# Moving one chunk of a key and value projection ahead of the output projection, and its k sums ahead of a residual and a norm

## The reference

```
x = x + xattn(ctx, layernorm(x), mask)
x = x + ffn(layernorm(x))

# xattn: latents l = layernorm(layernorm(x)), c = layernorm(ctx)
q    = l @ W_q
k, v = concat([c @ W_kv, l @ W_kv])        # 77 + 256 = 333 keys
qn, kn = rmsnorm(q) * scale, rmsnorm(k)    # per head of 64, 4 heads
attn = softmax(mask(qn @ kn.T)) @ v
out  = attn @ W_out + b_out

# ffn: shared part of 512 hidden units and 8 experts of 128, of which the router takes 2
out  = relu(x @ shared_up.T)**2 @ shared_down.T + sum_e w_e * relu(x @ up_e.T)**2 @ down_e.T
```

## Time and profile before

| | |
|---|---|
| median of 3 runs | 1163.17 us (1162.99 to 1163.61) |
| profiled execution, its own time | 1166.36 us |
| profiled execution, span of its instructions | 1164.6 us |
| PE busy | 1149.4 us (99% of the span) |
| DVE busy | 1005.6 us (86%) |
| ACT busy | 800.1 us (69%) |
| POOL busy | 542.9 us (47%) |
| mean granted TensorE clock | 0.994 |

### The profile page before, as it was taken

One profiled execution on the slowest core, in us unless ns is written; L12 is line 12 of the kernel. 1 busy time (PEld: TensorE's weight loads), 2 busy tenths in 40 slices (PEclk: granted clock), 3 DMA queues, 4 the chain that ended last, 5 costly groups with the idle time before them and its releaser, 6 DMA issues. The chain is left out here.

```text
span 1164.6 us, 32989 instructions
## 1 busy us (share of the span) xinstructions
PE 1149.4 (99%) x11772; PEld 1074.1 (92%) x11772; DVE 1005.6 (86%) x3511; ACT 800.1 (69%) x1896; POOL 542.9 (47%) x466
## 2 busy tenths in 40 slices
PE   7999999999999999999999999999999999999997
PEld 7799999999999999999999999999999999999997
DVE  6788888889988889988888988889888899888887
ACT  6567776676866667766677766678766678666673
POOL 3344545444545444445445444445454445454432
PEclk9899999999999999999999999999999999999999
DMA  5000000000000000000000000000000000000000
GB/s 186 2 14 23 23 23 11 23 14 24 22 23 10 23 14 22 24 22 11 14 23 23 23 19 16 13 22 23 22 12 22 14 23 22 23 10 24 2 10 19
DMA packets 28145, 26.06 MB, mean 22 GB/s; under 512 B 6544, under 2 KB 27440, under 8 KB 27984
## 3 DMA queue, kind: packets, MB, share of 16 engines
q1 hardware_dynamic: 27904, 23.83, 6.6%
q0 software_dynamic: 80, 0.14, 0.0%
HBM read 15.57 MB, written 8.39 MB: 21 GB/s over the span
## 5 line engine op out<-in xcount | busy, mean ns | idle before, releaser
L1311 POOL TENSOR_TENSOR hid_lo<-relu,hid_hi 128x512 fp32r<-128x512 f32 x191 | 246.7, 1292 | 251.8 <-DVE hid_hi L1069 167.2
L295 PE MATMUL down_ps<-down_hi,hid_hi 128*128 128x256 f32 x768 | 234.2, 305 | 2.8 <-DVE acc L1091 2.6
L1091 DVE SCALAR_TENSOR_TENSOR acc<-down_ps,route_w,acc 128x256 f32<-128x256 f32 x512 | 221.8, 475 | 6.9 <-PE down_ps L297 6.2
L295 PE MATMUL up_ps<-x_hi,up_hi 128*128 128x256 f32 x768 | 227.5, 296 | 0.0
L297 PE MATMUL down_ps<-down_hi,hid_lo 128*128 128x256 f32 x768 | 216.6, 282 | 0.0
L296 PE MATMUL down_ps<-down_lo,hid_hi 128*128 128x256 f32 x768 | 216.1, 281 | 0.0
L296 PE MATMUL up_ps<-x_lo,up_hi 128*128 128x256 f32 x768 | 214.9, 280 | 0.0
L297 PE MATMUL up_ps<-x_hi,up_lo 128*128 128x256 f32 x768 | 214.7, 280 | 0.0
L676 ACT ACTIVATE probs<-masked,neg_max,q_scale 128x333 f32<-128x333 f32 x256 | 168.1, 658 | 1.1 <-DVE neg_max L930 1.1
L723 ACT ACTIVATE relu_sb<-up_ps 128x512 f32<-128x512 f32 x192 | 113.6, 592 | 72.8 <-PE up_ps L297 69.5
L295 PEld LDWEIGHTS down_ps<-down_hi,hid_hi 128*128 128x128 f32 x768 | 144.9, 189 | 15.6 <-issue 15.1
(11 more groups left out here) (148 smaller groups left out, 2838.7 us busy)
## 6 DMA issues: line engine op xcount, KB each, us to landing
out<-acc SPq DMA_DIRECT2D x31, 256.0 KB, 2.2
x_first<-in_x SPq DMA_DIRECT2D x16, 256.0 KB, 2.8
w_stage<-in_x SPq DMA_DIRECT2D x16, 256.0 KB, 2.8
up_stage<-in_up_t SPq DMA_DIRECT2D x1, 1536.0 KB, 6.4
down_stage<-in_down_t SPq DMA_DIRECT2D x1, 1536.0 KB, 7.9
c_first<-in_ctx SPq DMA_DIRECT2D x16, 77.0 KB
w_stage<-in_ctx SPq DMA_DIRECT2D x16, 77.0 KB
w_stage<-in_w_kv SPq DMA_DIRECT2D x1, 512.0 KB, 5.0
```

Source lines behind the costliest of these rows:

```text
L295: nc.tensor.matmul(out_ap, s_hi, m_hi, start=first, stop=False)
L1091: nc.vector.scalar_tensor_tensor(acc[:, t, :], down_ps[:, (e + 1) % 2, t * D:(t + 1) * D], route_w[:, t, e:e + 1], acc[:, t, :], ALU.mult, ...
L1311: nc.gpsimd.tensor_tensor(hid_lo[:, p % HID_RING, :], relu2[:, p % 2, :], hid_hi[:, p % HID_RING, :], ALU.subtract).then_inc(hid_lo_done, 1)
```

## The change

On TensorE chunk 2 of the keys and values of the next element is projected directly behind chunk 1, ahead of both halves of the output projection. On DVE `k_norms` part 0 moves ahead of the two residual halves and the second norm's statistics. On POOL `k_scales` part 0 moves ahead of `rstd_second`. No instruction is added or removed, no DMA is moved, and ACT's order stays as it is.

```diff
@@ TensorE, step
                 ffn("down", 5)
                 project_kv(b + 1, 1)
+                project_kv(b + 1, 2)
                 project_out(b, 0, following)
                 project_out(b, 1, following)
-                project_kv(b + 1, 2)
                 project_kv(b + 1, 0)
                 project_q(b + 1)
                 ffn("down", 6)
@@ DVE, step
                 add(5)
                 if first:
                     down_parts(2)
+                k_norms(b + 1, 0, False)
                 residual_half(b, 0)
                 residual_half(b, 1)
                 layer_norm2(b, first)
-                k_norms(b + 1, 0, False)
                 normalize2(b, first)
                 k_norms(b + 1, 1, False)
@@ POOL, step
                     ln_low(b + 1)
                 low(5)
+                if following:
+                    k_scales(b + 1, 0, False)
                 rstd_second(b, first)
                 if following:
-                    k_scales(b + 1, 0, False)
                     k_scales(b + 1, 1, False)
```

## The result

The changed kernel takes 1199.41 us (1198.73 to 1199.88, 4 runs) against 1163.33 us for the kernel before (4 runs): a ratio of 1.0303, 95% interval 1.0290 to 1.0315. It is 36 us slower; 1195.0 was predicted, with a range of 1180 to 1206. On another chip, with more runs of the kernel before beside it, the same two stood at 1198.61 and 1164.57, ratio 1.0296 (1.0281 to 1.0311), 34 us.

A forecast was written before the change was run, and what follows sets the result against it. TensorE's in-order stream was taken to bound the kernel, the change acting only through late operands: 1.03 us in each of 31 steps, 32 us in all, gave 1195 us, range 1180 to 1206.

The forecast's parts named there:

- TensorE's order costs nothing by itself: On TensorE, out starts 1.38 us later and kv 2 1.55 earlier; the sum of its own work is unchanged, price nothing.
- The chain: K sums, residual, `var`, `rstd`, `x_hat`, part 1's k sums, `k_scale`, `k_rms` across DVE and POOL: TensorE 1.03 us late per step.
- The handover times: Signal delays between engines, 0.04 to 0.13 us for each of five handovers, uncertain by 0.25 us per step.
- The first wait: TensorE at `transpose_x2` waits for `x_hat`, starting 0.58 us late in each step.
- the second: TensorE at `transpose_k`'s fifth transpose waits for `k_rms` part 1: 1.03 us late, the wait at `transpose_x2` included.
- The first step: The step of `b` = 0, with its own 1.24 us wait for `k_rms`, charged the same 1.03 us as the others.
- the clock as a rival for each step: New TensorE waits halve the granted clock each step, 1.7 us per stretch, 51 us on top, 1246 us; 5%.
- The sum: Over the whole span, 31 steps at 1.03 us make 32 us, taken from the profiled execution to the median: 1195.2 us.
- only the first wait is paid: `k_rms` comes before TensorE needs it, so only `transpose_x2`'s 0.58 us per step is paid: 1181 us; 7%.
- POOL's results come before its records end: On POOL, 1.03 us of `rstd` and part 1's `k_scale` is only record, so time stays at 1163 us; 6%.
- The Trainium skill's rule on DVE's handovers: DVE's next instruction starts only once the pipeline ahead is empty: 0.17 us later per step, 5 us more, 1200 us.

The follow-up runs named there:

- POOL's order of before: Changed kernel with `rstd` put back ahead of both `k_scale` on POOL: 1205.19 us, ratio 1.0352 to the kernel before.
- both with the k sums between the halves: Changed kernel with part 0's k sums between the two residual halves: 1212.76 us; the same with `rstd` back ahead of `k_scale` on POOL: 1210.07 us.
- DVE's and POOL's parts alone: Kernel before with only the DVE and POOL moves of the change, TensorE's order kept: 1241.35 us, ratio 1.0654.
- POOL's alone: Kernel before with only `k_scale` part 0 moved ahead of `rstd` on POOL: 1226.26 us, ratio 1.0536.
- k sums of part 1 first: Changed kernel with `k_norms` part 1 moved ahead of `normalize2` on DVE: 1181.25 us, ratio 1.0134 to the kernel before.
- TensorE's part alone: Kernel before with only kv chunk 2 moved ahead of the output projection, DVE and POOL orders kept: 1186.65 us, ratio 1.0192.
- both edits together: Changed kernel with `k_norms` part 1 ahead of `normalize2` and `transpose_x2` behind down 7: 1187.14 us, ratio 1.0196 to the kernel before.

## Why the prediction was right

*TensorE's order costs nothing by itself.* Right. Out starts 588.50 - 582.34 = 6.16 us behind the block against 4.75 before, 1.41 later (1.38 predicted), and the period's growth is the two waits (0.49 + 0.52 us against 1.02), with the first step's clock beside it.

*The chain.* All its members in us from the start of the block at L411 (565.81 before, 582.34 after):

| | before | predicted | after |
|---|---|---|---|
| `k_sum` part 0 starts | 8.63 | 7.18 | 7.22 |
| residual starts | 5.96 | 7.99 | 8.02 |
| `var` ends | 8.12 | 10.15 | 10.19 |
| `x_hat` ends | 10.18 | 11.72 | 11.74 |
| `transpose_x2` starts | 11.22 | 11.80 | 11.79 |
| `k_rms` part 1 ends | 12.78 | 13.81 | 13.81 |
| fifth transpose starts | 12.86 | 13.89 | 13.87 |
| first scores start | 16.84 | 17.87 | 17.88 |

The handover times, read off single rows of the kernel before, held to 0.04 us in an order that had never run. The period grew by 1.02 us where 1.03 was the sum.

*The first wait is covered by the second.* "The first wait included" was right: with `transpose_x2` moved behind down 7 the period stays at 36.29. The split between the two was forecast as 0.58 and 0.45 and came out as 0.49 and 0.52.

*The first step.* Here a term was mis-sized. It was charged 1.03 like the others, and took 2.5 us more; with the order of before in it, 3.3 us come back. The 1.03 fits the waits of that step; what it lacked is the low stretch that was 6.7 us long in place of 3.4. The prediction had kept the clock as a rival for each step, at 1.7 us a stretch where the rows give about 1.5, and not asked about the one step in which it already fell. The steady steps never lost the clock, as the profile's row of 9s shows.

*The sum.* 30 x 1.02 + 2.5 is 33.1, and the span grew by 32.8, 0.3 having been gained before the first block. The medians differ by 36.1. The 3 us between are in the base: the profiled execution before was 3.0 us above its median of 1163.33, and that after 0.2 below its own. Carrying the sum from the profiled execution to the median assumed that both would stand alike to their medians. Why the profiled execution before stood above them is not shown. That, with the first step's 1.5 us, is why 1195.0 came out 4.4 us low.

*The rivals.* That only the first wait is paid is what the kernel does once the k sums of part 1 are moved as well (1181.25 us measured, 1181 worked out for the rival). That the clock falls in each step did not happen: from the second block to the last the granted clock is 1.00 in both kernels. That POOL's results come before its records end is refuted: `x_hat` starts at 593.34, 0.04 us behind the end of `rstd`, and DVE waits for it in 31 steps. The Trainium skill's rule on DVE's handovers (VectorE: DVE Perf Modes, The DRAIN you can't avoid) gave 1200, nearer to the median, but not for its reason: the residual starts at 590.36, still 0.09 us before `k_norm` ends at 590.45. The prediction had used only a part of that section: it goes on that a next instruction that isn't held starts earlier, and the rows of both traces are in line with that. That 1200 is near the median is luck; the first step and the base make up the distance.

None of these kernels beats the one before. There TensorE waits 1.6 us in 1164 for the operands that these edits move, so a better order of them has little to return; none was found that does.

## What to carry to other kernels

Where one in-order engine is the bound and hardly waits (here 1.6 us in 1164), an order change elsewhere has little to win and much to lose: find the operands that it takes latest, write down the margin of each (here 0.96 us for `x_hat` and none for `k_rms`), and walk the moved work through every queue up to them. A wait that is free today (DVE's 27 us for `k_scale`) is no reason to move its producer ahead, and work that looks movable may be what covers a latency (the k sums covered `rstd`). Of several waits on one chain only the last sets the time: fill a hole with what the chain needs next, not with other work.

## What the runs showed of the hardware that was not expected

The granted clock fell to 0.50 for 6.7 and 6.9 us behind the first step's waits in the two profiled executions of the changed kernel, and for 6.8 or 6.9 us in four experiments that keep most of that step (`transpose_x2` behind down 7, POOL's order of before, and both with the k sums between the halves). It fell for 3.4 us in the kernel before and in three others (DVE's and POOL's parts alone, POOL's alone, k sums of part 1 first), and not at all in the remaining three (TensorE's part alone, the first step as before, and both edits together). There is one profiled execution of each kernel but the changed one, so what sets the length is not shown; the longest waits don't go with the longest stretches, for DVE's and POOL's parts alone had 3.4 us. On one chip seven runs of the kernel before, unchanged, went from 1162.55 us (mean granted clock 0.999) to 1165.32 (0.996), and others at 0.994 lay between: a spread of 3 us in which the low stretches have a part and are not all of it.

POOL's `k_scale` of 111x8 took 1.72 us on the mean in the kernel before and 1.64 to 1.65 in all the others that were looked at. What makes the difference was not found; an overlap with DVE's `x_hat` exists with either duration.
